# Cross attention scores on 64 by 64 tiles of TensorE, one head to each half of the rows

## The chip, the cores and the metric

One core of a Trainium2 chip runs the whole program; nothing is shared with another core. The metric is the device time of one execution in microseconds (us), lower is better. The program is built ahead, and its inputs lie in HBM.

## The reference, cut to what matters

A latent array x of 8 batches of 64 rows by 256 passes through twelve layers: four groups of a cross attention, a self attention and a feed-forward layer. The change concerns the second cross attention (layer 1, `l1x`) and the fourth (layer 3, `l3x`), and no other layer. Both have 16 heads of 16 numbers, 64 queries and 1601 keys per batch; keys and values come from the context of each batch.

```
# layer 1
logits = (q @ k^T) / sqrt(16); masked keys are left out; softmax over the keys; @ v; @ W_proj + b
# layer 3
q = l2norm(x @ Wq + bq) * exp(min(scale_mul_log, log 100)); k = l2norm(y @ Wk)
attn = softmax(q @ k^T + attn_bias) ; out = attn @ (y @ Wv) @ Wo + bo
```

The mask of layer 1 is one per batch, query and key; the bias of layer 3 is one per query and key. Layer 1 keeps the masked logits at a value so low that their exponential is zero.

## The kernel before, in words

Both layers are built by `context_attention` (L2983), with `normed=False` for l1x and `normed=True` for l3x. Queries and keys are kept as sums of two f16 parts, high and low (`kh`, `kl` for the keys), and a score is the sum of three products, high by high, low by high, high by low. To do this in one matmul the three parts of a pair of heads lie above each other on the contracting rows: `kst` has 3 x 32 key rows and one row of a constant, `qst` the 96 query rows and one row that carries minus the maximum. The two heads of a pair (u, 8 of them) stand beside each other as 128 query columns, where the 16 rows of the other head are zeroed (`pair_mask`, L3499, L3663).

The work is written out as a plan of items. `prepared` runs once ahead of the loop; in the loop over the batches b and the 13 key tiles m of 128 keys, two steps stand in each tile (`steps`), and a step names the items of the next batch that are done in it (`at_step`). The loop over b = 7 has no next batch and so nearly no items.

- K: keys of 128 rows (c = 0 or 1) for 1024 or 577 keys, 6 matmuls for each bank (L3344). In l1x ACT makes `kh` (L3518) and DVE makes `kl` (L3685). In l3x the keys are normalized first (items N, I, U), and POOL makes both (L3273, L3275).
- V: values of four key tiles (L3360).
- Stacking: the SP queue waits until the low parts of a half c are made, then copies `kh`, `kl` and `kh` again into `kst`, three copies of 32 rows for each pair, 24 per batch (`stack`, L3192; the copies are L3200). The constant row of `kst` is written once by L3173. SP does this in program order with the load of the next context (L3211) and, in l1x, of the next mask (`load_mask`).
- A: the scores with queries on the partitions, for the maxima alone (L3371). An item is one pair and 1024 or 577 keys: 128 columns of weights, moving up to 512 keys. DVE adds mask or bias and takes the maximum over the keys in one instruction (L3711), reading two banks at once. A waits for the copies of its pair (`stacked[u]`).
- M: the maxima of four pairs are turned by four transposes (L3379), and ACT writes them as the last row of `qst` (L3546). All queries of a batch wait for both (`row_made`).
- `turned(b, m, g)`: the scores again, now with keys on the partitions, half g (four pairs, 512 query columns) at a time: four matmuls of 128 columns (L3417) into bank `S_BANK + g`. For the first four key tiles (`ON_VECTOR`) DVE adds the mask or bias (L3743, L3745) on the way to `pT`; for the other nine TensorE adds it by one matmul with a one-hot matrix (L3414). ACT takes the exponential (L3581).
- `values(b, m, g)`: 16 matmuls per key tile, weights of 17 columns (16 values and a one), on four column tiles of the array (L3433, each recorded as two passes for fp32).
- R, E, O, P: the result of the batch before is normalized, turned and projected.

The order on TensorE for a key tile m is: `turned(m, 0)`, the items of step 2m, `turned(m, 1)`, the items of step 2m + 1, then `values(m - 1)` for both halves. ACT and DVE do the items of the step before ahead of the exponential of a step (`step_before`). `turned(m, g)` waits for the exponential, or DVE's addition, of tile m - 1 and the same half. Items that need PSUM use two slots of two banks in turn: TensorE waits until the one before last in the same slot has been read.

```
for u, h: A = ("A", u, h)        # 8 pairs x 2 halves of the keys = 16 items per batch
steps of l1x: K at 0, 2, 3, 5; V at 6, 10, 13, 16; A from 8 to 23; M at 18 and 25
steps of l3x: K at 0, 1, 7, 8; N at 2, 3, 9, 10; V at 4, 6, 11, 14; A from 12 to 24; M at 20 and 25
```

## Time and profile before

| | us |
|---|---|
| median of 3 runs | 2508.22 (2506.53 to 2508.93) |
| profiled execution, its own time | 2501.07 |
| its span in the profile | 2499.3 |
| TensorE busy in the span | 2236.3 (89%) |
| VectorE (DVE) busy | 1650.0 (66%) |
| ScalarE (ACT) busy | 1243.2 (50%) |
| GpSimd (POOL) busy | 808.3 (32%) |

PE is TensorE's matmuls, PEld its weight loads, SPq the queue from which SyncE issues DMAs. A row of the timeline gives start, length, engine, line, operation, output and inputs, shapes and how many instructions of the kind are merged; its length runs from the first start to the last end. A matmul's duration holds its latency, so matmuls that follow each other overlap. "PEclk" is the granted clock of TensorE, 1.00 for 2.4 GHz and 0.50 for 1.2 GHz.

### The profile page before, as it was taken

How to read it: one execution, taken by the hardware profiler on the slowest of the kernel's cores; microseconds unless marked ns; L12 is line 12 of the kernel's file. 1: busy time of each engine (PE TensorE's matmuls, PEld its weight loads, DVE VectorE, ACT ScalarE, POOL GpSimd, SP SyncE). 2: the span in 40 equal slices, each digit the busy share in tenths (PEclk: the TensorE clock that was granted, in tenths of full speed). 3: DMA queues.
4: the chain of work that ended last, by engine and by line, in shares of the span. 5: the costliest groups of instructions: out<-in, count | busy, mean ns of one | idle time of the engine just before them, and what ended most of it. 6: DMA issues, size and time to landing. Idle time of an engine off the chain costs nothing. (4 is left out here: it accounts for less than half of the span.)

```text
span 2499.3 us, 50978 instructions
## 1 busy us (share of the span) xinstructions
PE 2236.3 (89%) x20593; PEld 1417.7 (57%) x20650; DVE 1650.0 (66%) x3182; ACT 1243.2 (50%) x2071; POOL 808.3 (32%) x660
## 2 busy tenths in 40 slices
PE   6885779999978889999999999699879999998898
PEld 4764445666654555656655666356546555566554
DVE  4987456555548756888888854644576666665577
ACT  2326234555554225555555554566436555563565
POOL 5610052233206112321233300045445455433254
PEclk8998899999989989999999999899999999999999
DMA  3200453423313047676776764133322323220231
GB/s 113 71 7 1 144 136 103 107 78 106 79 66 106 13 118 144 121 133 133 151 146 122 125 113 80 34 102 102 116 67 67 86 69 86 69 67 23 71 96 60
DMA packets 358618, 226.84 MB, mean 91 GB/s; under 512 B 289913, under 2 KB 326610, under 8 KB 358386
## 3 DMA queue, kind: packets, MB, share of 16 engines
q1 hardware_dynamic: 355314, 215.20, 35.5%
q0 software_dynamic: 3072, 8.39, 1.2%
q8 instruction: 165, 2.70, 0.4%
q14 instruction: 67, 0.55, 0.1%
HBM read 114.87 MB, written 0.52 MB: 46 GB/s over the span
## 5 line engine op out<-in xcount | busy, mean ns | idle before, releaser
L3950 POOL TENSOR_TENSOR l2x_rows<-l2x_rows,l2x_one 128x256 f16<-128x256 f32 (+1 forms) x91 | 89.2, 1006 | 379.6 <-DVE l2x_rows L1507 354.5
L100 PE MATMUL PS<-hot 128*128 128x512 f16 x460 | 134.3, 427 | 82.1 <-DVE l0a_g L1119 17.5
L4054 PE MATMUL PS<-l2x_rows,l2x_pth 128*128 128x512 f16 x832 | 200.3, 379 | 1.7 <-DVE l2x_mean L4263 1.7
L3711 DVE CUSTOM_DVE_ANT_0 l1x_junk<-PS,l1x_bias 128x1024 bf16<-128x1024 f32 (+1 forms) x128 | 123.2, 991 | 73.6 <-PE PS L3371 72.7
L4256 DVE TENSOR_TENSOR l2x_pl<-l2x_sc,l2x_ph 128x1664 f16<-128x1664 f32 x64 | 125.1, 1954 | 44.6 <-ACT l2x_ph L4133 43.9
L4151 ACT ACTIVATE l2x_meanT<-PS 128x256 f32<-128x256 f32 x64 | 24.5, 383 | 250.5 <-PE PS L4016 250.5
L4241 DVE CUSTOM_DVE_ANT_0 l2x_sc<-PS,l2x_bias 128x1665 f32<-128x1665 f32 x64 | 120.9, 1889 | 36.3 <-issue 35.0
L3711 DVE CUSTOM_DVE_ANT_0 l3x_junk<-PS,l3x_bias 128x1024 bf16<-128x1024 f32 (+1 forms) x128 | 123.6, 991 | 24.3 <-PE PS L3371 21.6
L4008 PE MATMUL PS<-l2x_kh,l2x_qth 128*128 128x512 f16 (+1 forms) x512 | 131.9, 339 | 1.5 <-issue 1.5
L4008 PE MATMUL PS<-l2x_kh,l2x_qtl 128*128 128x512 f16 (+1 forms) x512 | 131.9, 339 | 0.0
L4008 PE MATMUL PS<-l2x_kl,l2x_qth 128*128 128x512 f16 (+1 forms) x512 | 131.9, 339 | 0.0
L100 PEld LDWEIGHTS PS<-hot 128*128 128x128 f16 x460 | 44.8, 107 | 150.8 <-issue 35.7
L3581 ACT ACTIVATE l3x_pT<-PS 128x512 f32<-128x512 f32 x144 | 84.3, 592 | 91.9 <-PE PS L3417 88.7
L4054 PEld LDWEIGHTS PS<-l2x_rows,l2x_pth 128*128 128x128 f16 x832 | 79.4, 98 | 73.1 <-issue 3.3
L4126 ACT ACTIVATE l2x_sc<-l2x_sc,l2x_shift 128x1665 f32<-128x1665 f32 x64 | 107.9, 1686 | 19.5 <-DVE l2x_shift L4243 19.5
L3581 ACT ACTIVATE l1x_pT<-PS 128x512 f32<-128x512 f32 x144 | 83.3, 592 | 60.3 <-PE PS L3417 59.3
L4059 PE MATMUL PS<-l2x_rows,l2x_ptl 128*128 128x256 f16 x832 | 111.6, 273 | 0.0
L4133 ACT ACTIVATE l2x_ph<-l2x_sc 128x1664 f16<-128x1664 f32 x64 | 101.8, 1590 | 9.1 <-DMA l2x_pth<-l2x_ph 7.2
L1642 POOL TENSOR_TENSOR l2f_unit_l<-l2f_unit,l2f_unit_h 128x384 f16<-128x384 f32 x72 | 75.0, 1063 | 70.5 <-ACT l2f_unit L1634 70.5
L1642 POOL TENSOR_TENSOR l3f_unit_l<-l3f_unit,l3f_unit_h 128x384 f16<-128x384 f32 x68 | 73.5, 1102 | 70.2 <-ACT l3f_unit L1634 70.2
L4059 PEld LDWEIGHTS PS<-l2x_rows,l2x_ptl 128*128 128x128 f16 x832 | 81.5, 98 | 15.7
L3417 PE MATMUL PS<-l1x_qst,l1x_kst 97*128 97x128 f16 (+1 forms) x832 | 80.3, 219 | 5.6 <-issue 2.6
(866 smaller groups left out, 6109.0 us busy)
## 6 DMA issues: line engine op xcount, KB each, us to landing
l2f_unit<-in_L_ffn_units_dram SPq DMA_DIRECT2D x36, 384.0 KB, 3.1
l3f_unit<-in_L_ffn_units_dram SPq DMA_DIRECT2D x34, 384.0 KB, 3.0
l1x_kst<-l1x_kh SPq DMA_DIRECT2D x128, 100.1 KB, 2.2
l3x_kst<-l3x_kh SPq DMA_DIRECT2D x128, 100.1 KB, 2.2
l2x_rows<-in_ctx_dram SPq DMA_DIRECT2D x8, 1536.0 KB
l1x_ctx<-in_ctx_t_dram SPq DMA_DIRECT2D x7, 1601.0 KB, 7.3
l3x_ctx<-in_ctx_t_dram SPq DMA_DIRECT2D x7, 1601.0 KB, 7.0
l1x_kst<-l1x_kl SPq DMA_DIRECT2D x64, 100.1 KB, 2.2
```

Of the source, the lines that this page charges most:

```text
L100: self.nc.tensor.matmul(self.PS[:, bank, :], self.hot[:, 0:P], self.hot[:], start=True, stop=True)
L1642: last = self.k.nc.gpsimd.tensor_tensor(wl[:, at], w[:, at], wh[:, at], ALU.subtract)
L3581: nc.scalar.activation(to, of, ACT.Exp, scale=1.0 / S_SCALE).then_inc(exp_done, 1)
L3711: v.tensor_tensor_reduce(junk[:, slot(it), 0:n], slot_banks(it)[:, 0:n], bias[:, 0 if normed else b % 2, at:at + n], 1.0, LOWEST, ALU.add, ...
L3950: last = nc.gpsimd.tensor_tensor(high[:, at], of[:, at], one[0:p, at].unsqueeze(2).unsqueeze(3).to_broadcast([p, i, NC, P]), ALU.mult)
L4008: last = nc.tensor.matmul(PS[:, j, 0:n], x[:, d, r, :], y[:, b % 2, d, at:at + n], start=(e == 0), stop=(e == len(terms) - 1))
L4054: nc.tensor.matmul(PS[:, ACC, :], pth[:, u % 2, m, :], rows2[:, b % 2, :, :, m, :], start=(m == 0), stop=False)
L4059: last = nc.tensor.matmul(PS[:, ACC, 0:D], ptl[:, u % 2, m, :], rows2[:, b % 2, 0, :, m, :], start=False, stop=(m == KT - 1))
L4126: nc.scalar.activation(sc[:], sc[:], ACT.Exp, bias=shift[:, u % 2:u % 2 + 1], scale=1.0 / S_SCALE, accum_out=rsum[:, u % 4:u % 4 + 1]).the ...
L4133: nc.scalar.activation(ph[:], sc[:, 0:ODD], ACT.Copy).then_inc(p_high, 1)
L4241: link(v.tensor_tensor_reduce(sc[:], PS[:, 0:len(cols), :].rearrange("p b n -> p (b n)")[:, 0:KEYS], bias[:], 1.0, LOWEST, ALU.add, ALU.ma ...
L4256: v.tensor_tensor(pl[:], sc[:, 0:ODD], ph[:], ALU.subtract).then_inc(p_low, 1)
```

## The change

Each head has its own rows now. The 16 rows of high keys, 16 of low keys, the constant row and 16 rows of high keys (49 in all, `KROWS`) of the first head of a pair lie on partitions 0 to 48, those of the second on 64 to 112; `qst` alike, with 64 query columns instead of 128 and nothing zeroed. Every score matmul uses one 64 by 64 tile of the array: 49 rows, 64 columns.

- Stacking: six copies of 16 rows for each pair instead of three of 32 rows, 48 per batch; the constant row is written by two DMAs.
- A: an item is a quartet of heads (two pairs, v of 4) and 401 keys (j of 4): four matmuls of 401 columns on the four tiles, into two banks. DVE reads each bank by its own instruction. The first item of a quartet waits for the copies of both its pairs. 16 items per batch as before.
- M: two transposes instead of four, and two copies of one row by ACT.
- `turned(b, m)`: both halves at once, 32 matmuls of 64 columns; half g is now the g-th head of each pair, in bank `S_BANK + g`. It waits for both exponentials of the tile before.
- Mask and bias: in l1x TensorE adds the mask for all 13 key tiles, in four matmuls of 512 columns on the four tiles, and DVE and the turned mask (`bias_t`, `mask_t`, its DMA and POOL's conversion) are gone from it. In l3x DVE keeps the first four tiles; for the others the bias is two f16 terms on each half of the rows, eight matmuls.
- Order: TensorE does `turned(m)`, the items of both steps, the values. ACT does both exponentials of the tile and then the items of its two steps; DVE both additions and then the items.
- The queries are turned by f16 matmuls against an f16 identity, not by fp32 transposes, and copied once per pair. Heads are counted in another order in the values and in the output weights (on the host, before the launch).

```diff
-    A = [("A", u, h) for u in range(R) for h in range(NH)]
+    ROW, KROWS, QCOLS = 32, 3 * DH + 1, 64
+    CHUNK = -(-NK // 4)
+    A = [("A", v, j) for v in range(QV) for j in range(NCH)]
-    ON_VECTOR = list(range(4))
+    ON_VECTOR = list(range(4)) if normed else []
...
                     for j in range(RC):
-                        for g, part in enumerate((kh, kl, kh)):
-                            sp.dma_start(kst[g * F:(g + 1) * F, b % 2, c * RC + j, :],
-                                         part[j * F:(j + 1) * F, c, :]).then_inc(stacked[c * RC + j], 16)
+                        for r in range(2):
+                            of = slice(j * F + r * DH, j * F + (r + 1) * DH)
+                            for at, part in ((0, kh), (DH, kl), (ROW + 1, kh)):
+                                sp.dma_start(kst[r * S + at:r * S + at + DH, b % 2, c * RC + j, :],
+                                             part[of, c, :]).then_inc(stacked[c * RC + j], 16)
...
                     elif kind == "A":
                         if j == 0:
-                            pe.wait_ge(stacked[c], (b + 1) * STACK)
+                            pe.wait_ge(stacked[2 * c], (b + 1) * STACK)
+                            pe.wait_ge(stacked[2 * c + 1], (b + 1) * STACK)
-                        for i, at, n in pieces(*halves[j]):
-                            last = nc.tensor.matmul(PS[:, bank + i, 0:n], qst[0:3 * F, b, c, :, :],
-                                                    kst[0:3 * F, b % 2, c, at:at + n], start=True, stop=True)
+                        at, n = chunks[j]
+                        for i in range(2):
+                            for r in range(2):
+                                rows = slice(r * S, r * S + KROWS)
+                                last = nc.tensor.matmul(PS[i * S:(i + 1) * S, bank + r, 0:n], qst[rows, b, 2 * c + i, :],
+                                                        kst[rows, b % 2, 2 * c + i, at:at + n], start=True, stop=True)
...
-                def turned(b, m, g):
+                def turned(b, m):
...
-                            pe.wait_ge(exp_done, e - G2 + 1)
+                            pe.wait_ge(exp_done, e)
...
                     if on_tensor:
-                        of_bias = fsp[:, m * P:m * P + n] if normed else bias[:, b % 2, m * P:m * P + n]
-                        nc.tensor.matmul(PS[0:n, S_BANK + g, :], of_bias, one_hot[:], start=True, stop=False)
-                    for i in range(UG):
-                        u = g * UG + i
-                        last = nc.tensor.matmul(PS[0:n, S_BANK + g, i * P:(i + 1) * P], kst[:, b % 2, u, m * P:m * P + n],
-                                                qst[:, b, u, :, :], start=not on_tensor, stop=not on_tensor or i == UG - 1)
-                    last.then_inc(turned_made, 1)
+                        for x in range(2 if normed else 1):
+                            for at, w_ in keys:
+                                for r in range(2):
+                                    half = slice(r * S, (r + 1) * S)
+                                    of_bias = fsp[half, x, :] if normed else bias[half, b % 2, :]
+                                    nc.tensor.matmul(PS[at:at + w_, S_BANK + r, :], of_bias[:, m * P + at:m * P + at + w_], one_hot[half, :],
+                                                     start=(x == 0), stop=False, skip_group_check=True)
+                    for u in range(R):
+                        for at, w_ in keys:
+                            for r in range(2):
+                                rows = slice(r * S, r * S + KROWS)
+                                last = nc.tensor.matmul(PS[at:at + w_, S_BANK + r, u * S:(u + 1) * S],
+                                                        kst[rows, b % 2, u, m * P + at:m * P + at + w_], qst[rows, b, u, :],
+                                                        start=not on_tensor, stop=not on_tensor or u == R - 1, skip_group_check=True)
+                                if u == R - 1 and at == keys[-1][0]:
+                                    last.then_inc(turned_made, 1)
...
                 for b in range(B):
                     for m in range(KT):
+                        turned(b, m)
                         for g in range(G2):
-                            turned(b, m, g)
                             for it in at_step(b, m * G2 + g):
                                 item(it)
...
-                            for it in step_before(b, m * G2 + g):
+                            exp(b, m, g)
+                        for g in range(G2):
+                            for it in at_step(b, m * G2 + g):
                                 item(it)
-                            exp(b, m, g)
...
-                        v.tensor_tensor_reduce(junk[:, slot(it), 0:n], slot_banks(it)[:, 0:n],
-                                               bias[:, 0 if normed else b % 2, at:at + n], 1.0, LOWEST, ALU.add, ALU.max,
-                                               rmax[:, c, j:j + 1]).then_inc(read[slot(it)], 1)
+                        for r in range(2):
+                            last = v.tensor_tensor_reduce(junk[:, slot(it), r * BANK:r * BANK + n], PS[:, 2 * slot(it) + r, 0:n],
+                                                          bias[:, 0 if normed else b % 2, at:at + n], 1.0, LOWEST, ALU.add, ALU.max,
+                                                          rmax[:, r, c, j:j + 1])
+                        last.then_inc(read[slot(it)], 1)
```

In the plan the last items move a little: in l3x the last four A stand in steps 22 and 23 (before 22 to 24), and M of the second half in step 24 (before 25) in both.

## Rows read from the trace of the kernel before

**Rows 1.** The page's granted clock in 40 slices of 62.5 us.
```profile
PEclk8998899999989989999999999899999999999999
```

**Rows 2.** Windows by stage: length, busy time (instructions) of each engine, clock, DMA share, GB/s.
```profile
386.00:428.90 42.90, 41.26 (x669) 28.29 (x674) 25.27 (x50) 24.43 (x43) 11.18 (x3) 1.00 0.26 60
428.90:706.70 277.80, 257.15 (x4220) 176.38 (x4256) 155.20 (x315) 147.91 (x265) 75.81 (x34) 1.00 0.34 91
706.70:726.40 19.70, 18.48 (x508) 13.62 (x508) 5.47 (x10) 14.45 (x28) 0.00 (x0) 1.00 0.01 3
...
1863.70:1915.40 51.70, 48.52 (x691) 30.49 (x689) 35.24 (x58) 31.14 (x51) 25.57 (x15) 1.00 0.34 92
1915.40:2238.40 323.00, 299.48 (x4355) 189.50 (x4352) 210.92 (x363) 186.18 (x313) 141.71 (x88) 1.00 0.28 76
2238.40:2258.10 19.70, 18.95 (x512) 13.49 (x508) 5.46 (x10) 14.36 (x28) 19.53 (x3) 1.00 0.01 3
```

**Rows 3.** Waits in 428.9 to 706.7, then 1915.4 to 2238.4: total, times, longest.
```profile
PE PS L3344 <- DVE l1x_ticks L3688: 9.5, 6, 1.6
...
PE PS L3371 <- DVE l3x_rmax L3711: 7.6, 12, 0.6
```

**Rows 4.** Lines L3200 and L3173: ns min/median/max, first and last start; then landing.
```profile
L3200 SPq DMA_DIRECT2D l1x_kst<-l1x_kh x128: 507/594/1532, 346.1 to 683.9; - x128
...
DMA to landing us min/median/max: 2.1/2.2/3.9
...
L3173 SPq DMA_DIRECT2D l1x_kst<-l1x_kl x1: 607/607/607, 324.6 to 324.6; - x1
```

**Rows 5.** Timeline of the SP queue, one loop of l1x, first and last copies.
```profile
437.74 0.54 SPq L3200 DMA_DIRECT2D l1x_kst<-l1x_kh  x1
...
452.32 1.23 SPq L3200 DMA_DIRECT2D l1x_kst<-l1x_kh  x2
...
454.23 0.59 SPq L3200 DMA_DIRECT2D l1x_kst<-l1x_kh  x1
```

**Rows 6.** The same in one loop of l3x; the second row merges two copies around a wait.
```profile
1937.42 0.51 SPq L3200 DMA_DIRECT2D l3x_kst<-l3x_kh  x1
...
1945.00 8.62 SPq L3200 DMA_DIRECT2D l3x_kst<-l3x_kh  x2
```

**Rows 7.** One of eleven loads of another layer, line L2095.
```profile
L2095 SPq DMA_DIRECT2D l1a_pre_b<-_attn_pre_b_columns_dram x1: 432/432/432, 734.0 to 734.0; - x1
```

**Rows 8.** Timeline of DVE at an l1x loop's end; then the next loop's first scores.
```profile
471.20 1.23 DVE L3711 CUSTOM_DVE_ANT_0 l1x_junk<-PS,l1x_bias 128x1024 bf16<-128x1024 f32 x1 [0.34 <-PE PS L3371]
...
472.35 0.76 DVE L3711 CUSTOM_DVE_ANT_0 l1x_junk<-PS,l1x_bias 128x577 bf16<-128x577 f32 x1
473.03 0.08 DVE L3711 DVE_READ_ACCUMULATOR2_ANT l1x_rmax<- 128x1 f32 x1
...
474.57 0.40 PE L3417 MATMUL PS<-l1x_qst,l1x_kst 97*128 97x128 f16 x4
```

**Rows 9.** Timeline of the SP queue ahead of the l3x loop.
```profile
1849.34 0.51 SPq L3200 DMA_DIRECT2D l3x_kst<-l3x_kh  x1
```

**Rows 10.** Timeline of PE: l1x scores, maxima, values; then scores of the fourth self attention.
```profile
600.25 0.39 PE L3417 MATMUL PS<-l1x_qst,l1x_kst 97*128 97x128 f16 x4
600.48 0.41 PE L3371 MATMUL PS<-l1x_kst,l1x_qst 96*128 96x512 f16 x2
600.82 0.64 PE L3433 MATMUL PS<-l1x_pT,l1x_v 128*17 128x64 f32 x32
...
2300.09 0.20 PE L2789 MATMUL PS<-l3a_kh,l3a_qh 64*64 64x64 f16 x2
2300.12 0.20 PE L2789 MATMUL PS<-l3a_kl,l3a_qh 64*64 64x64 f16 x2
```

**Rows 11.** Timeline of ACT, last loop of l1x; then line L3581.
```profile
722.94 1.09 ACT L3581 ACTIVATE l1x_pT<-PS 128x512 f32<-128x512 f32 x2 [0.48 <-PE PS L3417]
...
724.50 1.09 ACT L3581 ACTIVATE l1x_pT<-PS 128x512 f32<-128x512 f32 x2 [0.48 <-PE PS L3417]
...
L3581 ACT ACTIVATE l1x_pT<-PS x144: 569/597/602, 402.1 to 726.6; 128x512 f32<-128x512 f32 x128, 65x512 f32<-65x512 f32 x16
```

**Rows 12.** Windows, ahead of the l3x loop: columns as in rows 2.
```profile
1824.00:1833.50 9.50, 7.00 (x24) 3.93 (x24) 5.18 (x8) 3.18 (x4) 0.00 (x0) 0.70 0.52 119
```

More of the change, by code:

```diff
@@ L2996, in context_attention @@
     G2 = 2
-    UG = R // G2
+    ROW = 32
+    KROWS = 3 * DH + 1
+    QCOLS = 64
+    CHUNK = -(-NK // 4)
+    chunks = [(at, min(CHUNK, NK - at)) for at in range(0, NK, CHUNK)]
+    NCH = len(chunks)
+    QV = R // 2
     VW = DH + 1
     Q4 = P // 4
-    HG = H // G2
     VT = 4
@@ L3324, in item @@
                             pe.wait_ge(q_dve, c)
[L3325 removed]
+                        pe.wait_ge(unit_made, 1)
+                        pe.wait_ge(q_blank, 1)
+                        for u in range(c * RC, (c + 1) * RC):
                             for t in range(NT):
[L3327 to L3328 removed]
+                                last = nc.tensor.matmul(PS[:, Q_BANK + u % RC, t * P:(t + 1) * P], q3[:, t, u, :], ident16[:],
+                                                        start=True, stop=True)
                         last.then_inc(q_turned, 1)
@@ L3411, in turned @@
                     on_tensor = m not in ON_VECTOR
+                    keys = [(at, min(S, n - at)) for at in range(0, n, S)]
                     if on_tensor:
-                        of_bias = fsp[:, m * P:m * P + n] if normed else bias[:, b % 2, m * P:m * P + n]
-                        nc.tensor.matmul(PS[0:n, S_BANK + g, :], of_bias, one_hot[:], start=True, stop=False)
-                    for i in range(UG):
-                        u = g * UG + i
-                        last = nc.tensor.matmul(PS[0:n, S_BANK + g, i * P:(i + 1) * P], kst[:, b % 2, u, m * P:m * P + n],
-                                                qst[:, b, u, :, :], start=not on_tensor,
-                                                stop=not on_tensor or i == UG - 1)
@@ L3642, in item @@
                                                  ALU.mult))
-                            last = three(q[:].rearrange("p t (r f) -> p t r f", r=R), SQ / NEAR)
+                            last = three(q[:], SQ / NEAR)
                         else:
@@ L3652, in item @@
                             st.wait(dve, "q_free")
-                            last = three(xn[:].rearrange("p t (r f) -> p t r f", r=R), SQ * float(DH) ** -0.5)
+                            last = three(xn[:], SQ * float(DH) ** -0.5)
                         st.end(last, "q_three")
@@ L3753, in _ @@
                                 add_bias(b, m, g)
-                            for it in step_before(b, m * G2 + g):
+                        for g in range(G2):
+                            for it in at_step(b, m * G2 + g):
                                 item(it)
```

159 lines of the change are left out of this document (74 added, 85 removed).

## The prediction

> **What bounds the kernel now.** I read the slices first: TensorE is near full in almost all of them and its clock is granted whole while the second and the fourth cross attention run [rows 1]. Then the windows, cut where the first transposed score tile of a batch starts [rows 2]. A batch of the second attention (l1x, L1_xattn) takes 42.9 us in its first loop, 277.8 / 6 = 46.3 us in the next six, and 19.7 us in the last, which makes no keys. In the fourth (l3x) the same are 51.7, 323.0 / 6 = 53.8 and 19.7 us. TensorE is busy 93% of the six loops in both. The waits agree: only 9.5 us and 7.6 us in six loops are its longest ones [rows 3]. So today both loops are bound by TensorE, and the copies that stack the keys (kst, the SP queue) are hidden.
>
> How well hidden they are is the question. The SP queue needs 0.59 us for one such copy and 2.2 us more until it has landed [rows 4]. In the l1x loop that starts at 428.9, the first copy goes out at 437.74, 8.9 us in, when the low halves of the first 128 key rows are made; the 24 copies end at 454.82, so 17.1 us, 0.71 each with the few long ones [rows 5]. In the l3x loop that starts at 1915.4 they begin 22.0 us in; 12 end at 1945.6 (8.2 us, 0.68 each), and the other 12 wait for POOL's second half until about 1953.07, 37.7 us in [rows 6]; in every other loop that is 39.1.
>
> **Copies.** Each pair of heads now needs 6 copies of 16 rows instead of 3 of 32, so 48 per batch instead of 24, with the same bytes, on the same SP queue. What does a 16-row copy cost there? The constant row goes out as 16 pieces of 3202 bytes, exactly the new shape, and took 607 ns against 594 ns for 32 rows [rows 4]. So the issue does not shrink with the rows. I take 0.69 us each between the two stretches above; bounds are 0.64 (the steady spacing, 1.23 us for two [rows 5]) and 0.71. The cheapest copies anywhere take 0.43 us [rows 7]; that is a rival. One mask copy of 0.6 us per batch goes away in l1x and is not on this path.
>
> Who waits: the maxima (items A) are issued on TensorE in program order, before the score tiles of the next key tile. A quartet v needs the copies of pairs 2v and 2v+1, so the last needs all 48. Behind the waiting TensorE stand all scores and values.
> - l1x: the last copy has landed at 8.9 + 48 x 0.69 + 2.2 = 44.2 us into the loop. Then come the last four items and the closing steps. An item is now two reductions of 401 columns. 1024 columns take 1.15 us start to start and 577 take 0.68 [rows 8], so 1.05 ns a column and 0.08 fixed: 0.50 each, 1.0 an item, 4.1 for four. The first matmuls and the latency before DVE add 0.4, and from the last reduction's end (473.03) to the next loop's first score (474.57) are 1.5 [rows 8]; I take 1.6. The loop takes 44.2 + 6.1 = 50.3, against 46.3: +4.0 x 6. In the first loop the copies start at 8.1: 49.5 against 42.9, +6.6. Sum **+30.6**.
> - l3x: the first 24 copies end at 22.1 + 16.6 = 38.7, so the second 24 start at 38.7 or 39.1, on average 38.9. Landed: 38.9 + 16.6 + 2.2 = 57.7. Here all four items stand in one key tile, so the tail is 5.7. The loop takes 63.4 against 53.8: +9.6 x 6; the first 63.2 against 51.7: +11.5. Sum **+69.1**.
> - Before the loops: in l3x the second half starts at 1849.34 [rows 9]. It has landed at 1849.3 + 16.6 + 2.2 = 1868.1, and with a tail of 6.1 the loop begins at 1874.2, not 1863.7: **+10.4**. In l1x 346.1 [rows 4] + 33.1 + 2.2 + 6.1 = 387.5, against 386.0: **+1.6**.
>
> **TensorE's own work.** Priced, though it is mostly hidden behind the copies. One 401-column quartet on four tiles is 0.17 + 3 small starts, 0.19 us, against 0.34 for 577 columns and 0.44 for 1024: 16 items were 5.3 us, now 3.0. Scores: before, 4 matmuls of 128 columns take 0.23 [rows 10], 0.46 per key tile. Now 32 matmuls of 64 columns. The fourth self attention starts two 64x64 tiles every 31 ns, on the diagonal; four column tiles of the values start 32 matmuls within 0.42 us (0.64 less the 0.22 of the last), 13 ns each, though fp32 streams twice as long [rows 10]. If four tiles run at once, 8 x 0.032 = 0.26 us; if only two, 0.50. I take 0.26, since the column tiles do run four abreast, and keep 0.50. The mask in l1x: from 2 x 0.22 on nine tiles to 0.22 on thirteen, -1.1 us a loop. In l3x two terms now go to both row halves, eight matmuls, 2 x 0.22 as before. Each change of tile shape costs about 0.1 us; there are 15 more in a batch. The sum is -2.3 -2.6 -1.1 + 1.5, with -0.5 for four fewer transposes: -5.0 us a loop in l1x, -3.9 in l3x. All of it turns into waiting for the copies, because the copies' start (keys in the first two to six key tiles) moves little: those tiles lose 0.2 for scores and gain about 0.1 for a switch and 0.2 for the mask. I leave the start where it is, +-1 us a loop.
>
> Against this stands the Trainium skill, TensorE: Matmul & The Clock Gate, section "Wait - 56ns, not 53.3ns?": starts of matmuls are never closer than some 25 ns, however few their columns. By that figure 32 score matmuls would take 0.8 us. This trace disagrees with it at 13 ns.
>
> **The wait between scores and exp.** Scores of both halves now come first, then both exps, then the next tile's scores, which need both exps; before, the halves alternated. In the last loop nothing covers this. A key tile takes 1.56 us there (724.50 less 722.94), with 0.60 for one exp of 512 [rows 11]. Now: mask 0.22 + scores 0.26 + latency 0.24 + two exps 1.2 + 0.05 = 1.97, +0.4 x 12 = **+4.8** in l1x; in l3x the mask is 0.44 in nine tiles, +0.6 each, and +0.3 in three: **+6.5**. In the other loops it hides behind the copies; without that cover a tile with maxima alone takes 2.0 instead of 2.25, and reductions (4 x 0.5) set the same floor.
>
> **Clock.** The granted clock is whole in both loops now [rows 2]. The new stalls are 5 us (l1x) and up to 8 us (l3x, before the third quartet). Where TensorE was busy 7.0 of 9.5 us, its clock averaged 0.70 [rows 12]. If it falls to 1.2 GHz, the first key or value item after the copies (2.6 us) can take up to 2.2 us more, with the transposes. I take 0.7 per loop: **+10**, between 0 and +31.
>
> **Sum.** 30.6 + 69.1 + 12.0 + 11.3 + 10 = +133 us. The profiled execution has 2499.3 us of span in 2501.1; after it: 2634. The median shown is 2508.2, 7.1 above that execution, so I forecast 2508.2 + 133 = **2641**.
>
> **Rivals.**
> 1. A 16-row copy is issued in less time: 0.43 us as [rows 7], 0.52 with spacing and long ones. For it: those copies exist; against it: the 607 ns row. Then l1x is free of the queue, and gains what the reductions leave, 2.6 us x 7 = -18, last loop +4.8. l3x: 38.4 + 12.6 + 2.2 + 5.7 = 58.9, +5.1 x 7 = +36, last loop and prologue +11.5. Sum +34: 2542.
> 2. Other side, faster: the queue costs nothing. It decides if a 16-row copy takes under 0.3 us (half the rows, half the time) and the keys come 1 to 2 us earlier, as in the first l3x loop, where the work before them was shorter. Then l3x is 36.5 + 7.2 + 2.2 + 5.7 = 51.6, -2.2 x 7 = -15, l1x -18, last loops +11: 2486. The same row speaks against it.
> 3. The forecast's queue, and TensorE slower too: four tiles don't run at once (+0.25 per key tile and +0.2 for the mask, 24 bare tiles +11; some 4 tiles before the copies start, +1.5 x 14 = +21) or the clock at its worst (+21): 2690.
> 4. Rivals 1 and 2 mixed so that l1x's gain cancels l3x's loss: no change, 2508.
>
> **Chances.** Forecast 0.68, rival 1 0.11, rival 2 0.09, rival 3 0.09, rival 4 0.03. The forecast's own range: 0.64 per copy takes 31 off and no clock loss 10; starts one us early or late are 14 either way, 0.71 adds 14: 2590 to 2680. To leave out no more than 0.2, the range reaches to rivals 1 and 3: **2540 to 2690**. Faster by over 0.2% (5 us, what a measurement of this kernel can tell): 0.09; within it 0.03; slower 0.88.
>
> **What would show it.** Right: 384 kst copies in each attention at some 0.6 us, loops of about 50 and 63 us, TensorE waiting for kst copies as its longest wait (near 5 and 11 us a loop), DVE with 401-column reductions of 0.5. Starts of 64x64 matmuls some 8 ns apart would confirm four tiles; 16 ns would be rival 3. Wrong: copies of 16 rows at 0.3 to 0.45 us, or loops under 46 and 54 us with TensorE still over 90% busy.

## The result, and the profile after

| | before | after |
|---|---|---|
| median, 4 runs each | 2507.38 us (2505.18 to 2508.93) | 2722.19 us (2716.62 to 2725.28) |
| span of the profiled execution | 2499.3 us | 2719.6 us |

The changed kernel takes 1.0855 of the time before, 95% interval 1.0835 to 1.0875: 215 us slower. The forecast was +133 (2641, range 2540 to 2690). The direction came as forecast, and the queue of the copies has its part in it; the size did not come.

Windows of the changed kernel, cut as in [rows 2] where each batch's first score tile starts; then its granted clock, as in [rows 1].
```profile
392.80:445.60 52.80, 42.04 (x1050) 27.37 (x1054) 21.36 (x74) 23.36 (x44) 13.60 (x5) 0.92 0.36 81
445.60:783.30 337.70, 280.66 (x6502) 176.21 (x6498) 132.12 (x459) 143.59 (x276) 67.93 (x25) 0.86 0.31 69
783.30:810.80 27.50, 21.59 (x854) 15.34 (x846) 0.50 (x2) 13.30 (x25) 0.00 (x0) 0.85 0.02 4
1957.60:2024.60 67.00, 53.71 (x1082) 32.14 (x1082) 34.66 (x90) 29.96 (x52) 26.05 (x15) 0.84 0.28 63
2024.60:2449.00 424.40, 340.45 (x6714) 202.95 (x6714) 215.09 (x555) 184.47 (x325) 149.91 (x88) 0.82 0.25 56
2449.00:2477.70 28.70, 22.16 (x872) 15.71 (x872) 5.55 (x10) 14.20 (x27) 14.75 (x3) 0.85 0.02 4
```
```profile
PEclk8998898878888989999999999999877788888999
```
The six middle loops now take 337.7 / 6 = 56.3 us in l1x (46.3 before, 50.3 forecast) and 424.4 / 6 = 70.7 us in l3x (53.8 before, 63.4 forecast). TensorE is busy 83% and 80% of them instead of 93%, and its clock, whole before, averages 0.86 and 0.82.

The longest waits of TensorE in the six loops of l1x, then of l3x; then line L3204, the key copies, with columns as in [rows 4].
```profile
PE PS L3380 <- DMA l1x_kst<-l1x_kh: 25.9, 15, 2.8
...
PE PS L3380 <- DMA l3x_kst<-l3x_kh: 45.8, 15, 6.8
```
```profile
L3204 SPq DMA_DIRECT2D l1x_kst<-l1x_kh x256: 507/589/1846, 352.1 to 771.5; - x128
L3204 SPq DMA_DIRECT2D l3x_kst<-l3x_kh x256: 507/590/2012, 1908.3 to 2433.9; - x128
...
who waited for it (us, times):
  PE PS L3380: 96.0, 40
...
DMA to landing us min/median/max: 2.1/2.2/4.0
```
A copy of 16 rows takes the queue 590 ns, as 32 rows did (594). TensorE's longest wait is now the one for kst, as forecast; before, it was for VectorE [rows 3]. But these waits, 25.9 / 6 = 4.3 and 7.6 us a loop (5 and 11 were forecast), don't make up the 10 and 17 us that a loop grew.

One l1x loop of the changed kernel, from its first score matmul at 557.95 to the next loop's at 615.23. First and last key copies in the timeline of the SP queue:
```profile
567.85 0.54 SPq L3204 DMA_DIRECT2D l1x_kst<-l1x_kh  x1
...
601.38 0.59 SPq L3204 DMA_DIRECT2D l1x_kst<-l1x_kh  x1
```
and TensorE from the last quartet of maxima on (L3380 maxima, L3451 values, L3428 mask, L3434 scores, L3388 the maxima's transposes), in the timeline:
```profile
605.03 0.89 PE L3380 MATMUL PS<-l1x_kst,l1x_qst 49*64 49x401 f16 x8 [1.73 <-DMA l1x_kst<-l1x_kh]
...
606.83 0.64 PE L3428 MATMUL PS<-l1x_one_hot,l1x_bias 64*64 64x512 bf16 x4
607.26 0.64 PE L3434 MATMUL PS<-l1x_qst,l1x_kst 49*64 49x64 f16 x32
607.70 0.86 PE L3380 MATMUL PS<-l1x_kst,l1x_qst 49*64 49x401 f16 x8
...
609.48 1.15 PE L3428 MATMUL PS<-l1x_one_hot,l1x_bias 64*64 64x512 bf16 x4
610.56 2.28 PE L3434 MATMUL PS<-l1x_qst,l1x_kst 49*64 49x64 f16 x32
612.77 0.46 PE L3388 MATMUL PS<-ident,l1x_both 128*97 128x128 f32 x2
613.16 0.64 PE L3451 MATMUL PS<-l1x_pT,l1x_v 128*17 128x64 f32 x32
614.83 0.64 PE L3428 MATMUL PS<-l1x_one_hot,l1x_bias 64*64 64x512 bf16 x4 [1.03 <-ACT l1x_pT L3599]
```
The copies start 567.85 - 557.95 = 9.9 us into the loop (forecast 8.9) and take 34.1 (33.1). The last quartet starts at 47.1 (44.2), and from there to the next loop are 10.2 us, where the forecast had 6.1. In this tail one row stands out: the last key tile's 32 score matmuls take 2.28 us (610.56), those of the tile before 0.64 (607.26). That tile has 65 keys, done as pieces of 64 and of 1 weight columns. By form, the 128 matmuls of one column in each attention have a row of their own:
```profile
L3434 PE MATMUL PS<-l1x_qst,l1x_kst 49*64 49x64 f16 x3200 | 59.7, 203 | 0.4 <-issue 0.3
...
L3434 PE MATMUL PS<-l1x_qst,l1x_kst 49*1 49x64 f16 x128 | 12.2, 188 | 0.0
```
Their own duration, 188 ns, is not longer; it is what goes on between them. In the last key tile of l1x's last loop the matmuls come in pairs, two of 64 columns, two of 1, two of 64. Three timelines of TensorE, each cut to a few ns there; a row is two pairs merged and starts where its first matmul does:
```profile
808.67 0.34 PE L3434 MATMUL PS<-l1x_qst,l1x_kst 49*64 49x64 f16 x4
...
808.81 0.34 PE L3434 MATMUL PS<-l1x_qst,l1x_kst 49*1 49x64 f16 x4
...
808.93 0.34 PE L3434 MATMUL PS<-l1x_qst,l1x_kst 49*64 49x64 f16 x4
```
A pair starts 0.12 to 0.14 us after the pair of the other width, in both directions; the two of a pair start 3 to 4 ns apart, those of 1 column too. So it is not the narrow matmul that takes long, but the change.

Mean time from a key tile's first score to the next one's, six middle loops, worked out from the starts of the score matmuls (us; the tiles not shown change by 0.5 or less, but for tile 6 of l1x, +1.1, and tile 7 of l3x, +1.8):

| key tile | 0 | 8 | 9 | 10 | 11 | 12 | whole loop |
|---|---|---|---|---|---|---|---|
| l1x before | 4.40 | 2.91 | 3.08 | 2.25 | 2.27 | 1.96 | 46.3 |
| l1x after | 5.93 | 3.77 | 4.08 | 5.30 | 3.14 | 4.64 | 56.3 |
| l3x before | 5.21 | 2.25 | 2.84 | 3.08 | 3.50 | 2.90 | 53.8 |
| l3x after | 6.96 | 2.54 | 8.71 | 4.83 | 7.38 | 4.66 | 70.7 |

The waits for copies lie where a quartet begins: in tiles 6, 8 and 10 of l1x (4.5, 5.6 and 15.4 us in six loops) and in tiles 7, 9 and 11 of l3x (9.2, 32.1 and 4.4). Tiles 12 and 0, the end of one batch and the beginning of the next, grow by 4.2 us in l1x and 3.5 in l3x without any wait for a copy.

### The profile page after: what moved, and what is told of

The parts are those of the page before. It is cut to its first block and busy times, and to the rows that moved or that the text cites. A ratio compares the mean times of both kernels' runs of the same rounds, so it can differ in the third digit from the quotient of the medians.

```text
span 2719.6 us, 64110 instructions
## 1 busy us (share of the span) xinstructions
PE 2324.4 (85%) x26810; PEld 1436.0 (53%) x26810; DVE 1618.7 (60%) x3622; ACT 1230.7 (45%) x2095; POOL 802.0 (29%) x655
## 5 line engine op out<-in xcount | busy, mean ns | idle before, releaser
L100 PE MATMUL PS<-hot 128*128 128x512 f16 x476 | 143.5, 441 | 81.5 <-DVE l0a_g L1119 17.5
L3730 DVE CUSTOM_DVE_ANT_0 l1x_junk<-PS,l1x_bias 128x401 bf16<-128x401 f32 (+1 forms) x256 | 133.7, 575 | 126.9 <-PE PS L3380 126.9
L3730 DVE CUSTOM_DVE_ANT_0 l3x_junk<-PS,l3x_bias 128x401 bf16<-128x401 f32 (+1 forms) x256 | 133.1, 574 | 98.4 <-PE PS L3380 97.5
L3599 ACT ACTIVATE l3x_pT<-PS 128x512 f32<-128x512 f32 x144 | 77.8, 591 | 219.2 <-PE PS L3434 219.2
L3599 ACT ACTIVATE l1x_pT<-PS 128x512 f32<-128x512 f32 (+1 forms) x208 | 112.7, 593 | 138.7 <-PE PS L3434 136.4
L3380 PE MATMUL PS<-l3x_kst,l3x_qst 49*64 49x401 f16 (+1 forms) x512 | 53.3, 434 | 86.6 <-DMA l3x_kst<-l3x_kh 55.7
L3256 POOL TENSOR_TENSOR l3x_tick<-ones 1x1 f32<-1x1 f32 x39 | 8.2, 211 | 322.0 <-DVE l3x_k L3721 320.6
L3703 DVE SCALAR_TENSOR_TENSOR l1x_kl<-PS,l1x_kh 128x1024 f16<-128x1024 f32 (+1 forms) x32 | 31.8, 994 | 117.9 <-ACT l1x_kh L3534 115.9
```

The costliest lines, as they stand in the source:

```text
L100: self.nc.tensor.matmul(self.PS[:, bank, :], self.hot[:, 0:P], self.hot[:], start=True, stop=True)
L3599: nc.scalar.activation(to, of, ACT.Exp, scale=1.0 / S_SCALE).then_inc(exp_done, 1)
L3730: last = v.tensor_tensor_reduce(junk[:, slot(it), r * BANK:r * BANK + n], PS[:, 2 * slot(it) + r, 0:n], bias[:, 0 if normed else b % 2, at ...
```

## The experiments

Ratios are to the kernel before, run on the same chip in turn with them. Its median was between 2502 and 2507 us on these chips, so a difference between the medians of two experiments is good to some 5 us. "Loops" are the means of the six middle ones, and a tile's time is read as in the table above.

**1. The copies alone, in the kernel before.**
```diff
                         for g, part in enumerate((kh, kl, kh)):
-                            sp.dma_start(kst[g * F:(g + 1) * F, b % 2, c * RC + j, :],
-                                         part[j * F:(j + 1) * F, c, :]).then_inc(stacked[c * RC + j], 16)
+                            for r in range(2):
+                                sp.dma_start(kst[g * F + r * DH:g * F + (r + 1) * DH, b % 2, c * RC + j, :],
+                                             part[j * F + r * DH:j * F + (r + 1) * DH, c, :]).then_inc(stacked[c * RC + j], 16)
```


> The kernel before, with one edit: in both cross attentions each 32-row copy of keys is issued as two copies of 16 rows, so the SP queue gets 48 copies a batch as in the changed kernel, and TensorE's, ScalarE's and VectorE's work stays as it was. Theory 1 (a copy costs the queue 0.69 us whatever its rows, and the queue then sets the loops): the l1x loops become about 8.9 + 33.1 + 2.2 + 5.5 = 49.7 us (from 46.3), the l3x loops about 62.5 (from 53.8), with first loops and the l3x prologue in all +95 us: about 2600 us. Theory 2 (the loss of the changed kernel comes from its tiles and its order, the copies are hidden): no change, 2508 us. In between: what is missing to the +215 us of the changed kernel after this run comes from the tail behind the copies, the tile shapes and the clock.

2594.1 us, 1.0333 (1.0306 to 1.036): +87. The loops take 47.8 us in l1x (49.7 expected) and 63.5 in l3x (62.5). The copies take 589 ns here too. The longest wait of TensorE in the six l3x loops:
```profile
PE PS L3372 <- DMA l3x_kst<-l3x_kh: 39.1, 23, 3.1
```
Theory 2 falls. The queue's price is near the forecast in sum, 1.9 us a loop under it in l1x and 1.0 over it in l3x. It leaves 128 us of the 215 to the rest, and to how the rest and the queue meet.

**2. Half of the copies left out, in the changed kernel.**
```diff
-                        for r in range(2):
+                        for r in range(2 if b < 2 else 1):
```
The waits for the copies count them accordingly.

> The changed kernel, with the key copies of the second head of each pair left out from the third batch on (its scores then use the keys of an earlier batch): 24 copies of 16 rows a batch instead of 48, in six loops of each attention; all else as it was. Theory 1 (the queue sets the loops): the six l1x loops fall from 56.3 us to some 44 to 48, the six l3x loops from 70.7 to some 52 to 57, in all about -150 to -190 us: 2535 to 2570. Theory 2 (slow tails, the piece of one key and the clock make the loss by themselves): they stay, and the gain is under 60 us: above 2660. Where the loops remain above those of the kernel before (46.3 and 53.8), the rest is a cost of the new tiles that does not pass through the queue.

2653.0 us, 1.0581 (1.0554 to 1.0608): -69, near theory 2 (a gain under 60) and far from theory 1. l1x loops 50.0, l3x loops 64.5. With 24 copies the queue is as it was before the change, yet the loops stay 3.7 and 10.7 us above those of before. In both, tile 12 still takes 4.6 us.

**3. The last key tile as one piece.**
```diff
-                    keys = [(at, min(S, n - at)) for at in range(0, n, S)]
+                    keys = [(at, min(S, n - at)) for at in range(0, n, S)] if n == P else [(0, n)]
```


> The changed kernel, where the last key tile (65 keys) is done as one piece of 65 weight columns instead of 64 and 1: 16 score matmuls instead of 32, all of the same shape, and half the mask matmuls of that tile. Theory 1 (the piece of one key changes the tile shape 16 times and takes 2.2 us instead of some 0.4, and stands in the tail before the maxima's transposes): -1.7 us in each of 16 batches, about -28 us: 2694. Theory 2 (it runs beside VectorE's reductions of the last quartet, which take 4 us): 0 to -5 us, 2717 to 2722, with at most the two last loops 1.7 us shorter.

2661.4 us, 1.0607 (1.0584 to 1.063): -61, twice what theory 1 gave. The end of one of its loops and the first rows of the next, timeline of TensorE:
```profile
545.28 0.42 PE L3434 MATMUL PS<-l1x_qst,l1x_kst 49*65 49x64 f16 x16
546.57 0.43 PE L3388 MATMUL PS<-ident,l1x_both 128*97 128x128 f32 x2 [0.87 <-issue]
...
547.90 0.41 PE L3428 MATMUL PS<-l1x_one_hot,l1x_bias 64*64 64x512 bf16 x4 [0.33 <-issue]
548.12 0.45 PE L3434 MATMUL PS<-l1x_qst,l1x_kst 49*64 49x64 f16 x32
```
Tile 12 falls from 4.64 to 2.75 us in l1x and from 4.66 to 2.65 in l3x. Tile 11, which ends with the mask or bias matmuls of the last tile (half as many now), falls by 0.8 in both. In sum the tail, from the last quartet's start to the next loop, falls from 10.0 to 7.4 us in l1x and from 10.8 to 7.6 in l3x: (2.6 + 3.2) x 6 = 35 us in the twelve middle loops, 6 in the two first ones. The other large part is in tile 0, 5.93 to 4.03 and 6.96 to 6.18: (1.9 + 0.8) x 6 = 16 us. Windows of tile 0, first two of the changed kernel, then two of this one (columns as above, the clock third from the end):
```profile
502.40:508.30 5.90, 5.90 (x118) 2.98 (x111) 0.36 (x1) 2.34 (x4) 0.00 (x0) 0.78 0.13 38
557.80:563.20 5.40, 5.40 (x48) 2.15 (x40) 0.00 (x0) 1.09 (x2) 0.00 (x0) 0.51 0.15 38
```
```profile
496.30:500.30 4.00, 4.00 (x88) 2.07 (x86) 0.00 (x0) 1.82 (x3) 0.00 (x0) 1.00 0.39 126
548.10:552.10 4.00, 4.00 (x96) 2.13 (x92) 0.00 (x0) 1.88 (x3) 0.00 (x0) 1.00 0.32 94
```
TensorE was busy all of tile 0 in all four; after the slow tile it is granted 0.78 and 0.51 of its clock there, without it 1.00. So the next batch's keys are made later, and its copies, which pace the loop, start 8.6 to 10.2 us into the l1x loop instead of 7.5 (8.3 in one loop). The last quartet starts as much earlier, at 44.3 instead of 46.3 us. The loops fall to 51.7 us in l1x and 66.7 in l3x, 1.4 and 3.3 above the forecast.

**4. All 32 matmuls of one shape.** This separates the shape from the number of matmuls.
```diff
-                        for at, w_ in keys:
+                        for at in (0, S):
+                            first_key = min(m * P + at, NK - S)
...
-                                    kst[rows, b % 2, u, m * P + at:m * P + at + w_], qst[rows, b, u, :],
+                                    kst[rows, b % 2, u, first_key:first_key + S], qst[rows, b, u, :],
```


> The changed kernel; in the last key tile the second piece of the score matmuls has 64 weight columns like all others, not 1: it reads the last 64 keys, so the last key's scores are those of another key. 32 matmuls as before the edit, but all of one shape. The mask matmuls of that tile keep their 64 and 1. Theory 1 (it is the change of tile shape from one matmul to the next that makes the 32 score matmuls take 2.2 us, and the stall it adds lets the clock fall): they take 0.4 to 0.5 us, and the time falls nearly as with one piece of 65 columns, by 50 to 60 us: 2665 to 2675. Theory 2 (it is the number of matmuls, 32 instead of 16, behind a stall at half clock): 2722.

2665.7 us, 1.0638 (1.0622 to 1.0654): -56. The last key tile of l1x's last loop, in this kernel and then in the changed one:
```profile
784.57 0.45 PE L3435 MATMUL PS<-l1x_qst,l1x_kst 49*64 49x64 f16 x32
```
```profile
808.67 2.21 PE L3434 MATMUL PS<-l1x_qst,l1x_kst 49*64 49x64 f16 x32
```
Same number of matmuls, 0.45 us against 2.21: the shape decides. A head pair is two matmuls of 64 columns and two of 1, so eight pairs have 16 changes of shape, with the one from the mask's matmuls: (2.21 - 0.45) / 16 = 0.11 us each.

**5. Both repairs of the diagnosis, and the floor.** Half of the copies left out and the tile in one piece; then all copies left out from the third batch on.

> The changed kernel, with both edits at once: the key copies of the second head of each pair left out from the third batch on (24 copies of 16 rows a batch; its scores then use the keys of an earlier batch), and the last key tile as one piece of 65 columns. Each alone took 69 and 61 us off 2722. Theory A (two separate prices, copies and the piece of one key, that add up): about 2722 - 69 - 61 = 2592, with l1x loops of 46.5 us and l3x loops of 61. Theory B (each hid behind the other, so that with both gone the time falls by more, to the kernel before less what TensorE saves): 2500 to 2540, l1x loops of 43 us, l3x loops of 53. Theory C (both are one and the same stall): 2645. What is left over 2508 belongs to the wait for six copies by a quartet, to the order of scores and exp, or to the clock.

2588.7 us, 1.0341 (1.0319 to 1.0362): theory A to within 4 us. The prices add. l1x loops 46.0, l3x 60.6.

> The changed kernel with the last key tile in one piece, and with all key copies left out from the third batch on (its scores use the keys of earlier batches): the loops as the new tiles and the new order would run them if copies were free. With half of the copies this was 2589, with l1x loops of 46.0 and l3x loops of 60.6 us. Theory 1 (what was left in l3x there, 60.6 against 53.8, is the third quartet's wait for its copies, since it needs six that start 40 us into the loop, where before one item needed three): l3x loops fall to some 54 to 56 us, l1x stays at 44.5 to 46, about 2550. Theory 2 (it is the new order, VectorE's reductions and the clock): l3x stays at 59 or above, 2575 or more. The tiles' own gain, if there is one, shows as loops under 46.3 and 53.8.

2565.8 us, 1.0245 (1.0216 to 1.0274). l1x stays at 46.2, l3x falls to 57.4: between the two theories. What was left of the third quartet's wait was worth 3.2 us a loop (tile 9: 5.94 to 3.13). But without a single copy, l3x is 3.6 us a loop above the kernel before, l1x level with it. TensorE's longest wait in the six l3x loops is then
```profile
PE PS L3381 <- DVE l3x_rmax L3731: 16.2, 24, 1.0
```
that is for VectorE's reductions, 2.7 us a loop (7.6 / 6 = 1.3 before [rows 3]). Tile 11, which has four maxima items (eight reductions of 0.50 us), takes 5.29 us against 3.50 before. TensorE's clock is not whole here either, 0.92 in these loops, and the last stretch, from the last reduction to the next loop, takes 2.5 to 3.1 us where it took 1.5 before. The new tiles save TensorE work, but no loop is clearly shorter by it.

**6. The order alone, in the kernel before.**
```diff
                         for g in range(G2):
                             turned(b, m, g)
+                        for g in range(G2):
                             for it in at_step(b, m * G2 + g):
```
and likewise on ScalarE and VectorE: both exps (both additions), then the items.

> The kernel before, with the order of the changed one alone: scores of both halves of a key tile first, then both exps, then the items, on TensorE, ScalarE and VectorE; tiles, copies and shapes as before. Theory 1 (the next tile's scores now need both exps, and the alternation was worth something): key tiles with nothing beside them go from 1.56 us to mask 0.44 + scores 0.46 + 0.24 + exps 1.2 = 2.3, +0.75 x 12 in each last loop, and the five or six tiles of a loop that take 2.0 to 2.3 us now rise by some 0.1 to 0.3: +18 and +20, about 2545 us. Theory 2 (it hides behind TensorE's items): only the two last loops, +15: 2523. Theory 3 (it costs nothing, or the later exps free the items): within 5 us of 2508.

2523.9 us, 1.008 (1.0057 to 1.0103): about +20, between theories 1 and 2 and nearer to 2 by the size, against both by the place. Tiles in the last loops stay at 1.56 us, so nothing was lost there, where both put a loss; instead the middle loops grow, 46.3 to 47.0 and 53.8 to 56.1 (tile 12: +0.45 in both), and the first ones by 3 us.

**7. The mask alone, in the kernel before.**
```diff
-    ON_VECTOR = list(range(4))
+    ON_VECTOR = list(range(4)) if normed else []
```


> The kernel before, with one part of the change alone: in the second attention the mask is added by TensorE in all thirteen key tiles (before, VectorE adds it in the first four); tiles, copies, order as before. TensorE gets 8 mask matmuls of 0.22 us more in each batch, 1.8 us, in key tiles 0 to 3, and VectorE 8 additions less. Theory 1 (these tiles are bound by TensorE's key and value items): +1.8 x 7 plus nothing in the last loop, where the exps bind, +12 us: 2519. Theory 2 (VectorE's addition was on the path between scores and exp, so both cancel): within 5 us of 2507. Theory 3 (VectorE frees the items earlier): 2490 to 2500.

2516.4 us, 1.0046 (1.0033 to 1.006): +11.5, theory 1. In the profiled execution the l1x loops grow by 0.6 us each and the first by 1.3, 5 us in all. Of the rest, 3.3 us lie ahead of l1x's first loop and 2.8 between the start of its last loop and l3x's first; what made them is open.

**8. TensorE kept busy while it waits.**
```diff
+                            if b > 0 and c >= 2:
+                                k.warm(bank, 16 if normed else 8)
                             pe.wait_ge(stacked[2 * c], (b + 1) * STACK)
```


> The changed kernel, with matmuls of no use put ahead of the wait for the copies of the third and fourth quartet (8 in l1x, 16 in l3x, each time into the bank that the waiting item writes afterwards), so that part of the stall is filled and the granted clock stays higher. Theory 1 (the loss holds a clock term: after the stall key and value items run at 1.2 GHz and delay the copies of the next batch): the granted clock of the six loops rises from 0.86 and 0.82 by some 0.05 to 0.1, and the time falls by 15 to 40 us: 2680 to 2705. Theory 2 (the queue paces the loops whatever the clock): within 5 us of 2722. The matmuls end after the copies have landed: above 2722 by what they overshoot.

2722.6 us, 1.0862 (1.0834 to 1.0891): nothing in sum. The six middle loops:
```profile
444.80:773.70 328.90, 288.16 (x6598) 179.62 (x6594) 131.54 (x459) 143.45 (x276) 68.02 (x25) 0.94 0.32 72
2015.80:2448.40 432.60, 371.51 (x6909) 215.49 (x6909) 214.99 (x555) 184.45 (x325) 151.85 (x89) 0.89 0.25 55
```
The clock rises from 0.86 to 0.94 and from 0.82 to 0.89. l1x gains 328.9 against 337.7, 8.8 us; l3x loses 8.2 (tile 11: 7.38 to 9.97 us). The place tells more than the sum. In l1x the last quartet starts as before, at 46.2 us, and the tail takes 8.6 us instead of 10.0. Such a tail in the changed kernel, then in this one:
```profile
605.00:615.20 10.20, 9.14 (x190) 5.26 (x194) 4.31 (x17) 3.11 (x7) 4.78 (x3) 0.67 0.45 162
```
```profile
545.10:553.80 8.70, 7.57 (x192) 4.67 (x195) 4.22 (x17) 3.11 (x7) 3.42 (x3) 0.87 0.54 189
```
In l3x the tail shortens too, from 10.8 to 9.2, but its last quartet starts at 62.9 us instead of 60.0, behind 16 matmuls of no use that run past the landing. So the part of the clock that came back is worth 1.4 to 1.5 us in a tail, 8 to 9 us in each attention.

**9. Half of the copies on another queue, nothing left out.** First on ScalarE's:
```diff
+                    elif kind == "C":
...
+                        for at, part in ((S, kh), (S + DH, kl), (S + ROW + 1, kh)):
+                            nc.scalar.dma_start(kst[at:at + DH, b % 2, c * RC + j, :],
+                                                part[of, c, :]).then_inc(stacked[c * RC + j], 16)
```


> The changed kernel, nothing left out: the 24 copies of the second heads of a batch are issued by ScalarE's queue, three behind each other at eight places of its program, the other 24 stay on the SP queue. Theory 1 (a copy costs issue time of its queue, whatever its size; the DMA engines have room): the last copies land as early as with 24 copies, so the time falls about as far as in the run that left half of them out, to some 2650 us, less what ScalarE's own issuing delays the exps (24 x 0.05 to 24 x 0.6 us a loop, beside a ScalarE that is under half busy). Theory 2 (the copies share the DMA engines and it is their transfer that takes 0.69 us): spacing on each queue doubles, and the time stays at 2722 or above.

> The changed kernel with both repairs, nothing left out: half of the copies on ScalarE's queue, and the last key tile as one piece of 65 columns. If the prices add: 2650 - 61, about 2590 us. If the order of scores and exps and the late quartet of copies were nothing, it would come below the kernel before, 2508 less some 20. Above 2640: ScalarE's issuing holds up the exps.

2744.7 us, 1.0984 (1.0945 to 1.1024), and with the tile in one piece 2687.2, 1.0736 (1.0714 to 1.0759): both worse than with all copies on SP (2722, 2661). The number is that of theory 2, its mechanism is not: a copy still takes SP 590 ns (median), so nothing doubled. The issue costs the same there, but on an engine that has work behind it: line L3580, and a row of ScalarE's waits in four l1x loops of the first of the two runs (501.6 to 743.5),
```profile
L3580 ACTq DMA_DIRECT2D l1x_kst<-l1x_kh x112: 514/611/1647, 400.6 to 785.6; - x112
```
```profile
ACT l1x_pT L3611 <- issue: 28.0, 8, 4.8
```
so an exp stands up to 4.8 us behind the copies, and TensorE's next scores behind the exp. Tile 4 of l1x takes 6.5 us instead of 2.0. The l3x loops did not suffer: 70.8 and 66.2 us against 70.7 and 66.7.

Then on POOL's queue, with the tile in one piece:
```diff
+                        for at, part in ((S, kh), (S + DH, kl), (S + ROW + 1, kh)):
+                            nc.gpsimd.dma_start(kst[at:at + DH, b % 2, c * RC + j, :],
+                                                part[of, c, :]).then_inc(second[c * RC + j], 16)
```


> The changed kernel, nothing left out: the copies of the second heads are issued by POOL's queue from the second batch on (24 a batch, 24 stay on the SP queue), and the last key tile is one piece. On ScalarE's queue a copy took 0.61 us of ScalarE's own time and the exps paid for it; POOL is idle 70% of l1x and 60% of l3x. If POOL issues one in some 1 us and the DMA engines have room: copies end before the loops need them in l1x (46 to 48 us a loop), and at about 52 us into the l3x loop (61 to 63 us), in all about 2600, against 2661 with all copies on SP. If POOL takes 1.5 us or more for one, its own casts and low halves come late, and it is 2661 or more. It beats the kernel before in neither case.

2591.4 us, 1.034 (1.0318 to 1.0362): as fast as with half of the copies left out (2588.7), with all of them made. l1x loops 47.0, l3x 61.9. The line of POOL's copies:
```profile
L3279 POOL DMA_DIRECT2D l3x_kst<-l3x_kh x112: 487/487/561, 1910.1 to 2304.9; - x112
```
POOL issues one in 0.49 us, half of what was guessed. The Trainium skill (DMA: Bandwidth & Descriptors, "Issuing engines are not separate DMA queues") says that issuing from several engines saves only the time that the issuing takes. The two runs agree: here that time was the bound, and the saving counted where the second issuer had time to spare.

This is the fastest version of the changed kernel that leaves nothing out. It takes back some 130 of the 215 us and stays 3.4% above the kernel before. No run beat that one, and the floor without copies (2566) says that faster copies in the middle loops alone can't.

## Why the direction was right and the size wrong

- **The copies' price: right.** 0.69 us was taken; 34.1 / 48 = 0.71 in the loop shown, 590 ns against 594, landing after 2.2. In the kernel before, the same copies cost +87 us where +95 was expected.
- **Four tiles at once: right.** 32 score matmuls take 0.42 to 0.45 us from the first start to the last end at the full clock, 0.19 of it the last one: (0.45 - 0.19) / 31 = 8 ns between starts. Rival 3's two at a time is out, and so is the Trainium skill's figure of some 25 ns that the prediction set against it (TensorE: Matmul & The Clock Gate, "Wait — 56ns, not 53.3ns?").
- **The tail behind the last quartet: the step that failed.** It was put at 6.1 us in l1x and 5.7 in l3x; it is 10.0 and 10.8. Its first part, up to the end of the last reduction, was put at 4.5 and 4.1 and takes about 5.3 and 4.6. The term that was far off is the closing one, from there to the next loop: 1.6 us was taken, read off the kernel before [rows 8], and it is 4.3 to 4.9 in l1x and 5.6 to 6.5 in l3x. Two things fill it, and the next two points are theirs.
- **The piece of one key, in the tail.** The prediction priced a change of tile shape at 0.1 us, and that is what one costs (0.11). But it counted "15 more in a batch", about one for each key tile, as its "0.1 for a switch" in the first tiles shows, and put them with TensorE's work that hides behind the copies. It missed the 16 of the last key tile, between the pieces of 64 and of 1, and that this tile stands behind the last copy: in the loop shown its scores start at 610.56, when the last reduction is done. Of 82 us missing, this one piece is 61: 41 in the tails, 16 in the tiles 0 behind them.
- **The clock, in the tail.** With the tile in one piece the six loops are 51.7 and 66.7 us, against 50.3 and 63.4: (1.4 + 3.3) x 6 = 28 above. In l1x that is the tail, 7.4 against 6.1. In l3x it is the tail, 7.6 against 5.7, and the last quartet's start, at 59.1 on average where 57.7 was forecast. TensorE's granted clock is low there: 0.67 in the l1x tail of the changed kernel (the eighth experiment shows it), behind an idle 1.7 us for the copies, and 0.54 in an l3x tail with the tile in one piece (2120.9 to 2128.4), with idle 2.6 us for the copies ahead of it and 1.0 and 0.4 for the reductions in it. Two neighbouring l3x loops of the fifth experiment's first run show the price; from the last quartet's start to the next loop,
```profile
2189.00:2196.70 7.70, 6.08 (x122) 3.35 (x110) 4.22 (x17) 2.95 (x7) 0.00 (x0) 0.53 0.51 200
2246.80:2253.20 6.40, 4.39 (x122) 2.70 (x107) 4.22 (x17) 2.97 (x7) 0.00 (x0) 0.82 0.01 3
```
with 122 matmuls recorded in each. In the first, the values, the bias and the scores of the last key tile run at half clock and end after the last reduction, and the closing part takes 3.1 us; in the second it takes 1.9. The prediction had a clock term, 0.7 us a loop for the next batch's key and value items, but none in the tail. The eighth experiment agrees: with the clock partly kept, the tails are 1.4 to 1.5 us shorter. The shortest tails of that fifth run are 6.3 us in l1x and 6.4 in l3x; what they have over the forecast, 0.2 and 0.7 us, was not tested.
- **What the tail does to the next batch: not seen.** The prediction let the l1x copies start at 8.9 us, as before. They start at 8.6 to 10.2, and mostly at 7.5 once the slow tile is gone, since tile 0 then runs at the whole clock. They pace the loop, so this is paid in full. The clock was priced as 10 us of TensorE's time; it should have been priced as a shift of the queue's start and a longer tail as well.
- **Ahead of the loops.** The l1x loop starts 6.8 us later than in the profile before, where +1.6 was forecast. With the order alone or the mask alone, which leave the work ahead of the loops as it was, it starts at 390.6 and 389.3, against 386.0; so some 4 of this may be no effect of the change.
- **The order: right where it was looked for, and not hidden elsewhere.** +11.3 was forecast for the last loops alone (for l3x, 6.5; the terms given there add up to 6.3). In the changed kernel the bare key tile takes 1.86 us in l1x (forecast 1.97) and 2.07 in l3x (2.19), near the forecast; the last loops grow by 7.8 and 9.0 us, the slow tile among it. But the order alone, in the kernel before, costs 20 us in the middle and first loops, where the prediction put nothing.
- **TensorE's saving of 5.0 and 3.9 us a loop: no gain, as forecast, but not for the reason given.** It was said to turn into waiting for copies. Without copies it does not come back: l1x is level, and the order and the mask cost 0.7 and 0.6 us a loop there by their own runs, so some 1.3 of saving may be hidden under them. l3x is 3.6 us slower, of which the order explains 2.2 by its own run. The remaining 1.4 may be VectorE's reductions, whose waits grew by as much, or the clock in the tail; no run took either away.
- **Rivals.** 1 and 2 (cheaper copies, free copies) are out by the 590 ns row. Of rival 3, the half with two tiles at a time is out, and the half with a dearer clock is borne out in kind. Rival 2's 2486 would not have come true with free copies either, since the floor is 2566 with the first batches' copies still in it.

The account by the ratios, in the order in which the parts were taken away: 62 us for the piece of one key, 67 for the second half of the copies and 24 for the first half, each good to some 8 us. That leaves 61 us over the kernel before: the copies of the first two batches, the order, the mask, and VectorE or the clock in l3x. The clock has no line of its own here; its share is in all of them.

## What to carry to other kernels

Count changes of tile shape per instruction, not per stage: a remainder of one column, alternated with full pieces, cost 61 us here, and one wider piece or one of the full width removes it. When a queue paces a loop, everything between its last transfer and the next batch's first work is paid in full, and so is all that delays its next start. A wait also costs what the lower clock behind it takes, if work on the path stands there. Before splitting a transfer, look at whether its issue shrinks with its size; if it does not, a second queue helps only on an engine that has nothing waiting behind it.

## What the runs showed of the hardware

- A change between 64-column and 1-column weight tiles cost 0.11 us each, in both directions, though the matmuls' own duration fell from 203 to 188 ns; matmuls of 1 column that followed each other started 3 to 4 ns apart. The Trainium skill (TensorEngine Tiling (Array Packing), "Key Properties") says that changing the tiling mode drains TensorE; the rows here agree, if 64 and 1 columns are two such modes, and put a number on it.
- Copies of 16 rows by 3202 bytes take 0.59 us of the SP queue, 0.61 of ScalarE's and 0.49 of POOL's.
- 16 matmuls with 65 weight columns (two tiles abreast) and 32 with 64 (four abreast) take the same 0.42 to 0.45 us at the whole clock.
- The l3x tail of 122 matmuls, with the tile in one piece and half of the copies, took 7.7 us at a granted clock of 0.53 and 6.4 at 0.82.
